# Channel order, first loads and first products of a two-stage layer on one core

## What is computed

```
qkv = xn @ W_qkv + b_qkv            # 512 -> 3 * 512, 16 heads of 32
q', k' = relu(q), relu(k), each times cos and sin of the position
kv = sum over rows of k'^T v        # per head, cos part and sin part
attn = (q' kv) / (q' sum(k') + 1e-4)
out1 = attn @ W_out + b_out
probs = softmax(xn @ choice_w^T)    # 8 experts
per batch and expert: its top 1024 rows -> silu(xn w1) w2, times the probability, added into the rows
```

## Time and profile before

| | us |
|---|---|
| median of 3 runs | 2501.93 (2501.14 to 2505.41) |
| the profiled execution, its time | 2501.82 |
| its span | 2500.0 |
| PE busy (matmul) | 2398.0 (96% of the span) |
| DVE busy | 1342.9 (54%) |
| ACT busy | 831.2 (33%) |
| POOL busy | 1078.0 (43%) |
| share of PE in the chain that ended last | 84% |

### The profile page before, as it was taken

The page is one execution under the profiler, slowest core; times in us unless marked ns, Lnnn a source line. Parts: engine busy times, 40 slices in busy tenths (PEclk is TensorE's granted clock), DMA queues, the critical chain, the costliest instruction groups (busy, mean ns, idle before and its releaser), DMA issues.

```text
span 2500.0 us, 34669 instructions
## 1 busy us (share of the span) xinstructions
PE 2398.0 (96%) x12544; PEld 2012.5 (80%) x12544; DVE 1342.9 (54%) x2654; ACT 831.2 (33%) x1458; POOL 1078.0 (43%) x959
## 2 busy tenths in 40 slices
PE   8999999999999999999999999998998999999898
PEld 7889988898999887777777787787787787787677
DVE  7777777687787795434335245245245344335331
ACT  4545544445454552222213213223223222223111
POOL 0100034200002565664565565565566566466541
PEclk9999999999999999999999999999999999999999
DMA  7555434455544455224224224323323323332222
GB/s 197 160 134 135 109 54 74 69 136 151 134 118 83 60 89 123 49 41 111 48 46 107 50 48 94 56 51 78 76 49 75 77 51 77 72 50 47 37 39 30
DMA packets 125947, 205.38 MB, mean 82 GB/s; under 512 B 28264, under 2 KB 53480, under 8 KB 125552
## 3 DMA queue, kind: packets, MB, share of 16 engines
q0 software_dynamic: 57088, 118.02, 26.5%
q1 hardware_dynamic: 68720, 85.42, 11.6%
HBM read 119.22 MB, written 100.93 MB: 88 GB/s over the span
## 4 chain that ended last, share of the span: by engine, by line
PE 84%; issue 6%; DVE 5%; another core or an unknown queue 2%; DMA 1%; ACT 1%; POOL 0%; POOLq 0%; DVEq 0%; SPq 0%; ACTq 0%
PE ps L1355 27%; PE ps L1357 26%; PE ps L1356 26%; PE ps L1448 2%; DVE h_lo L1322 1%; PE ps L1585 1%; DVE h_hi L1320 1%; DMA xo<-in_L_attn_x_dram 1%; PE ps L1382 1%; DMA normed_rows<-xo 0%; DVE one_lo L907 0%; ACT hf L773 0%; DVE stats L811 0%; DVE w_lo L1326 0%
## 5 line engine op out<-in xcount | busy, mean ns | idle before, releaser
L461 POOL DMA_INDIRECT rows<-normed_rows,idx_row x512 | 539.0, 1053 | 156.5 <-issue 156.5
L1355 PE MATMUL ps<-w_hi,h_hi 128*128 128x512 f32 x1024 | 412.7, 403 | 42.2 <-DVE h_lo L1322 21.0
L571 POOL DMA_INDIRECT out_dram<-y,idx x128 | 227.1, 1774 | 482.1 <-ACT y L793 480.0
L1355 PE MATMUL ps<-xi_hi,w_hi 128*128 128x512 f32 x1024 | 407.4, 398 | 8.5 <-issue 8.3
L1356 PE MATMUL ps<-w_lo,h_hi 128*128 128x512 f32 x1024 | 406.6, 397 | 5.8 <-issue 5.7
L1357 PE MATMUL ps<-w_hi,h_lo 128*128 128x512 f32 x1024 | 406.2, 397 | 4.6 <-issue 4.4
L1320 DVE CAST h_hi<-hf 128x512 fp32r<-128x512 f32 x256 | 111.3, 435 | 556.6 <-issue 292.2
L1356 PE MATMUL ps<-xi_lo,w_hi 128*128 128x512 f32 x1024 | 403.0, 394 | 1.6 <-issue 1.6
L1357 PE MATMUL ps<-xi_hi,w_lo 128*128 128x512 f32 x1024 | 401.5, 392 | 0.0
L773 ACT ACTIVATE hf<-ps 128x512 f32<-128x512 f32 x256 | 153.0, 598 | 678.5 <-PE ps L1357 437.6
L1355 PEld LDWEIGHTS ps<-w_hi,h_hi 128*128 128x128 f32 x1024 | 196.9, 192 | 96.8 <-issue 30.4
(11 more groups left out here) (176 smaller groups left out, 4117.3 us busy)
## 6 DMA issues: line engine op xcount, KB each, us to landing
xo<-in_L_attn_x_dram SPq DMA_DIRECT2D x32, 512.0 KB, 4.6
normed_rows<-xo SPq DMA_DIRECT2D x32, 512.0 KB, 4.9
out_dram<-bo POOLq DMA_DIRECT2D x16, 1024.0 KB, 9.1
out_dram<-xo POOLq DMA_DIRECT2D x64, 256.0 KB, 3.9
w_raw<-in_L_ffn_w_dram SPq DMA_DIRECT2D x32, 512.0 KB
w_raw<-in_L_ffn_w_dram SPq DMA_DIRECT2D x8, 2048.0 KB, 9.4
xn<-normed_rows SPq DMA_DIRECT2D x96, 128.0 KB, 2.5
rows<-normed_rows,idx_row POOLq DMA_INDIRECT x512
```

Source lines behind the costliest of these rows:

```text
L461: nc.gpsimd.indirect_dma_start(rows[:, tt, a, :], None, pieces[:, :], bass.IndirectOffsetOnAxis(ap=idx_row[:, b, tile, a:a + 1], axis=0)). ...
L571: nc.gpsimd.indirect_dma_start(of[:, :], bass.IndirectOffsetOnAxis(ap=idx[:, u * TPB + tt:u * TPB + tt + 1], axis=0), y[:, tt, :], None, c ...
L1355: nc.tensor.matmul(dst, a_hi, b_hi, start=start, stop=False, skip_group_check=True)
```

## The change

Channel c now lies in block k = c mod 4 at partition c div 4, so four neighbouring rows of a weight matrix belong to one partition, and each matrix is one transfer to 128 partitions. The two transposes on DVE read, and the write of xn scatters, in steps of that order: DVE reads every fourth element (16 bytes apart) where it read runs of 32, and `norm_rows` writes neighbouring elements 512 bytes apart.

The rest is order. The 19 increments leave SP and go to the engines that wait on them, x is loaded as two tiles and a half, Wk comes before the table and the biases, and q's bias has its own semaphore. At the start the statistics of half 1 and its normalisation move between the casts of weights; TensorE turns tiles 0 and 1, makes the left halves of the q products (256 columns) with tiles 2 and 3 turned between, and then the right halves, in banks 5, 6, 3 and 4. In block 0 of batch 0 the normalisation of block 1's half 0 moves from before the first tile to behind it.

```diff
-            for signal in (mm_done, kv_done, vv_ready, q_read, k_read, v_read, lg_read, o_raw, otr_done, out_done, fin, list_pe, idx_ready,
-                           silu_done, h_ready, down_done, y_ready):
-                sp.sem_inc(signal, AHEAD)
-            sp.sem_inc(prob_stored, DMA_AHEAD)
-            sp.sem_inc(wo_free, NBLK // 2 - 1)
...
-                for i in range(HPG):
-                    sp.dma_start(raw_weights(part)[i * HD:(i + 1) * HD, :, :],
-                                 w_qkv[i * P:(i + 1) * P, part * D:(part + 1) * D].rearrange("(k j) d -> j k d", j=HD)
-                                 ).then_inc(w_in[part], 16)
...
-            load_x(0, 0)
+                sp.dma_start(raw_weights(part), w_qkv[:, part * D:(part + 1) * D].rearrange("(p k) d -> p k d", k=KD)
+                             ).then_inc(w_in[part], 16)
...
+            for tt, landed in ((0, x_first), (1, x_in[0])):
+                sp.dma_start(x_half[0][:, tt, :], xf[tt * P:(tt + 1) * P, :]).then_inc(landed, 16)
             load_x(0, 1)
             sp.dma_start(ident, consts[:, C_IDENT:C_BLOCK]).then_inc(ident_in, 16)
             sp.dma_start(ch_rows, choice_w[:, :]).then_inc(ch_in, 16)
             load_weights(Q)
-            sp.dma_start(con[:, C_BLOCK:C_END], consts[:, C_BLOCK:C_END]).then_inc(table_in, 16)
             load_weights(V)
...
+            load_weights(K)
+            sp.dma_start(con[:, C_BLOCK:C_END], consts[:, C_BLOCK:C_END]).then_inc(table_in, 16)
+            sp.dma_start(bk[:, :], b_qkv[D:2 * D].rearrange("(a d) -> a d", a=1).to_broadcast([P, D])).then_inc(con_in, 16)
...
-                for i in range(HPG):
-                    sp.dma_start(w1_raw[i * HD:(i + 1) * HD, :, :],
-                                 w1[bass.ds(e, 1), i * P:(i + 1) * P, :].rearrange("e (k p) f -> p (e k) f", p=HD)
-                                 ).then_inc(w1_in, 16)
+                sp.dma_start(w1_raw[:, :, :], w1[bass.ds(e, 1), :, :].rearrange("e (p k) f -> p (e k) f", k=KD)
+                             ).then_inc(w1_in, 16)
...
+            for signal in (q_read, v_read, lg_read, fin, silu_done, y_ready):
+                act.sem_inc(signal, AHEAD)
             sqrt(0, 0)
-            sqrt(0, 1)
             def q_weights(m):
                 sl = slice(m * P, (m + 1) * P)
...
-            turned_hi(0, 0, None, 4)
-            turned_hi(0, 1, None, 5)
+            turned_hi(0, 0, None, X_BANKS[0])
+            turned_hi(0, 1, None, X_BANKS[1])
+            q_weights(1)
             act.wait_ge(ch_turned, 1)
             nc.scalar.copy(wq_hi[:, :, 3 * D:3 * D + E], ch).then_inc(ch_hi_ready, 1)
-            q_weights(1)
-            turned_hi(0, 2, None, 6)
-            turned_hi(0, 3, None, 7)
+            sqrt(0, 1)
             q_weights(2)
             q_weights(3)
+            turned_hi(0, 2, None, X_BANKS[2])
+            turned_hi(0, 3, None, X_BANKS[3])
...
                 def first_block(n):
                     q_out(n, 0, 0, 5, 1)
-                    q_out(n, 0, 1, 6, 2)
                     if n == 0:
                         kv_weights(K)
-                    q_out(n, 0, 2, 5, 3)
+                    q_out(n, 0, 1, 6, 2)
+                    q_out(n, 0, 2, FIRST_Q[2] if n == 0 else 5, 3)
                     q_out(n, 0, 3, 4, 4)
-                    sqrt(n + 1, 0)
+                    if n > 0:
+                        sqrt(n + 1, 0)
+                    else:
+                        act.wait_ge(table_in, 16)
...
                         k_high(n, t)
+                        if n == 0 and t == 0:
+                            sqrt(n + 1, 0)
...
-                            xn[:, 2 * s + tt, :].rearrange("p (k i j) -> p i k j", k=KD, i=HPG),
-                            src[:, tt, :].rearrange("p (i k j) -> p i k j", k=KD, i=HPG), mv[:, s, tt, 0:1],
+                            xn[:, 2 * s + tt, :].rearrange("p (k c) -> p c k", k=KD),
+                            src[:, tt, :].rearrange("p (c k) -> p c k", k=KD), mv[:, s, tt, 0:1],
...
                     xT_raw.rearrange("p k (a r) -> p a k r", a=HPG),
-                    xn[:, t, :].rearrange("p (a k j) -> p a k j", a=HPG, k=KD)).then_inc(pieces_turned, 1)
+                    xn[:, t, :].rearrange("p (a j k) -> p a k j", a=HPG, k=KD)).then_inc(pieces_turned, 1)
...
-                                    rows[:, tt, :, :].rearrange("p a (k j) -> p a k j", k=KD)
+                                    rows[:, tt, :, :].rearrange("p a (j k) -> p a k j", k=KD)
...
-            norm_half(0, 0, 0, False)
-            norm_half(0, 1, 0, False)
+            for signal in (vv_ready, k_read, o_raw, idx_ready, h_ready):
+                dve.sem_inc(signal, AHEAD)
...
+            dve.wait_ge(x_first, 16)
+            tile_stats(0, 0)
+            dve.wait_ge(x_in[0], 16)
+            tile_stats(0, 1)
+            half_stats(0)
+            dve.wait_ge(x_in[1], 16)
+            tile_stats(1, 0)
+            norm_rows(0, 0, 0, False)
+            tile_stats(1, 1)
             q_weights(0)
-            turned_lo(0, 0, 4)
-            turned_lo(0, 1, 5)
+            turned_lo(0, 0, X_BANKS[0])
+            turned_lo(0, 1, X_BANKS[1])
+            half_stats(1)
             dve.wait_ge(ch_hi_ready, 1)
             nc.vector.tensor_tensor(wq_lo[:, :, 3 * D:3 * D + E], ch, wq_hi[:, :, 3 * D:3 * D + E].bitcast(F32),
                                     ALU.subtract)
             q_weights(1)
-            turned_lo(0, 2, 6)
-            turned_lo(0, 3, 7)
+            norm_rows(0, 1, 0, False)
             q_weights(2)
+            turned_lo(0, 2, X_BANKS[2])
+            turned_lo(0, 3, X_BANKS[3])
+            q_weights(3)
             norm_store(0)
-            q_weights(3)
             norm_store(1)
...
                 n_first = b * NBLK
-                norm_half(n_first + 1, 0, 2 * b + 1, False)
+                if b > 0:
+                    norm_half(n_first + 1, 0, 2 * b + 1, False)
                 for t in range(TPB):
...
                     k_low(n_first, t)
                     if t == 0:
+                        if b == 0:
+                            norm_half(n_first + 1, 0, 2 * b + 1, False)
                         norm_stats(n_first + 1, 1)
...
+            for signal in (mm_done, kv_done, otr_done, out_done, list_pe, down_done):
+                pe.sem_inc(signal, AHEAD)
             pe.wait_ge(ident_in, 16)
-            for t in range(TPB):
-                turn_x(0, t, 4 + t)
-                if t == 1:
-                    pe.wait_ge(ch_perm_ready, 1)
-                    for k in range(KD):
-                        last = nc.tensor.transpose(ch[:, k, :], ch_perm[:, k * P:(k + 1) * P], ident[0:E, 0:E])
-                    last.then_inc(ch_turned, 1)
+            for t in range(2):
...
                 q_half(0, 5, 0)
+                if b == 0:
+                    pe.wait_ge(w_ready, 2)
+                    q_half(1, FIRST_Q[1], 0)
+                    for t in range(2, TPB):
+                        turn_x(0, t, X_BANKS[t])
+                    for m in range(2, KD):
+                        pe.wait_ge(w_ready, m + 1)
+                        q_half(m, FIRST_Q[m], 0)
                 pe.wait_ge(xT_ready, b * NBLK * TPB + TPB)
                 def block(n, first):
                     pe.wait_ge(xT_ready, (n + 1) * TPB)
                     q_half(0, 5, 1)
-                    if first:
-                        pe.wait_ge(w_ready, KD)
+                    if not first:
+                        kv(n - 1, TPB - 1)
+                    if first and b == 0:
+                        for m in range(1, KD):
+                            q_half(m, FIRST_Q[m], 1)
                     else:
-                        kv(n - 1, TPB - 1)
-                    pe.wait_ge(lg_read, AHEAD + n * TPB)
-                    q_rest(1, 6)
-                    pe.wait_ge(q_read, AHEAD + n * KD + 1)
-                    q_rest(2, 5)
-                    pe.wait_ge(k_read, AHEAD + n * TPB)
-                    if first and b > 0:
-                        pe.wait_ge(fin, AHEAD + b * NT)
-                        pe.wait_ge(rank_out, b)
-                    q_rest(3, 4)
+                        pe.wait_ge(lg_read, AHEAD + n * TPB)
+                        q_rest(1, 6)
+                        pe.wait_ge(q_read, AHEAD + n * KD + 1)
+                        q_rest(2, 5)
+                        pe.wait_ge(k_read, AHEAD + n * TPB)
+                        if first:
+                            pe.wait_ge(fin, AHEAD + b * NT)
+                            pe.wait_ge(rank_out, b)
+                        q_rest(3, 4)
```

More of the change, by code:

```diff
@@ L54 @@
 VW = P + HPG
-CON_LOADS = 3
+CON_LOADS = 2
 HALF = D // 2
@@ L58 @@
 AHEAD, DMA_AHEAD = 1, 16
+X_BANKS = (0, 1, 2, 7)
+FIRST_Q = (5, 6, 3, 4)
 XN_TILES = B * NBLK * TPB
@@ L427, in _ @@
                 load_w2(e + 1)
-            sp.wait_ge(w1_in, HPG * 16 * E)
+            sp.wait_ge(w1_in, 16 * E)
             sp.wait_ge(w2_in, 16 * E)
```

(25 more changed lines are left out.)

26 lines of the change are left out of this document (14 added, 12 removed).

## The result

The changed kernel takes 2540.18 us, median of 6 runs (2537.2 to 2556.68), against 2505.43 for the kernel before beside it (2501.14 to 2509.13): ratio 1.0155, 95% interval 1.0126 to 1.0184. Its profiled execution took 2539.84 us with a span of 2538.0, 38.0 longer than before's span. The forecast was 2503.5.

What follows compares the result with a forecast made beforehand. The prediction took TensorE's stream as the bound. 2501.8 us, plus 1.1 net for the start and 0.5 for strided transposes, gave 2503.4 (2503.5 in terms of the median), range 2498.8 to 2507.0.

Steps and rivals of the forecast that it cites:

- something in stage 3 shifts: Unnamed case: something in stage 3, such as gathers beside a faster w1, shifts either way by several us; chance 0.05.
- Wq at 8.8, by the rate of x: Start: Wq, loaded at x's 380 GB/s, is there at 8.8 us instead of about 12.
- The third rival: Start: loads to 128 partitions no faster than 223 GB/s, Wq at 11 us, 2506 us in all; chance 0.06.
- First turning at 8.1: Start: TensorE turns the first tile of x at 8.1 us, 4.3 to 4.4 us after statistics can begin.
- First product at 11.5: Start: TensorE's first q product begins at 11.5 us, 4.5 earlier than before.
- q phase 14.0 us: First block's q products: 14.0 us instead of 12.13, from added turning, a longer slow pace and a wait for Wq.
- V at 25.5: First block: the first v product starts at 25.5 us instead of 28.16, a gain of 2.66.
- V + 32.0, and 0.7 for the writes: Block 1's right half: DVE's list ends 32.0 us after the first v product, strided writes add 0.7: 58.2 against 57.09.
- Writes at 0.72: `norm_rows` on DVE: each strided write of xn takes 0.72 us, between 0.54 and 0.83.
- Transposes +0.4: DVE's transposes in stages 1 and 3: reading every 16 bytes adds 0.4 us each, between 0 and 0.44.
- Coming through, +0.5: Blocks 2 and 3 of batch 0: DVE's gaps do not hide all the slower transposes; +0.5 us reaches the total.
- The strided transposes bound stage 1: Rival: slower transposes exceed the 1.18 us a steady tile leaves free on DVE; +20 us, 2522; chance 0.05.

Runs made afterwards that it cites:

- the second run of the norm first: Changed kernel, 24 increments at TensorE's start, second block's norm before the first tiles, first `norm_rows` before the wait for half 1: 2497.85 us, ratio 0.9962.
- the one that has increments directly ahead of the loop: Changed kernel with 24 unread semaphore increments directly ahead of TensorE's expert loop: 2497.57 us in one run, on a chip where the kernel before takes 2505.58.
- 24 and 52: Changed kernel with that many unread semaphore increments at the start of TensorE's program: 2380.92 and 2383.36 us, the kernel before at 2375.59.
- 64 and 76: Kernel before with that many unread semaphore increments at TensorE's start: 2523.18 us (2505.58 without, on that chip) and 2402.66 us (2375.59 without).

## Why the prediction was wrong

The forecast of 2503.5 us is 37 too low. The step that failed is the one that costs stage 3 at nothing. It asked what the change does to stage 3's data (slower transposes "off the path", single transfers of w1 "issued long before their casts") and, since no instruction of TensorE changes there, nothing of its code. What changed is where they lie. The case "something in stage 3 shifts" had 0.05 and no place in the trace; its place is the loop's head, its price 4.3 us a pass in this trace (3.7 to 4.3 in those of the other kernels that wait at the second product). Nothing in before's trace shows the border, though the order of instructions shows that 36 products were added ahead of the loop, and the queue of instruction packets (98 of them) that the loop is fetched anew.

Point by point:
- *SP's first load near 0.8:* 0.75. Right.
- *Wq at 8.8, by the rate of x:* cast at 9.28. Nearly right; from 8 to 9 us the loads to 128 partitions moved 397 GB/s, where the four transfers had 223. The third rival's cause is wrong, though V and block 1's right half came out where it put them (28 and 60.7), for other reasons.
- *First turning at 8.1:* 9.57, as before. Wrong. "The added statistics and its wait for half 1" were sized at 0.2 us; the rows of half 1 came at 6.48, and the reciprocal, whose root was there at 5.5, stood behind them until 7.09.
- *First product at 11.5:* 13.00, 1.5 late like the turning. That wait is only part of it: with `norm_rows` ahead of it (the second run of the norm first, 11.94) the first product gained 0.5 and the turning, at 8.44, 0.6; and one multiplication of the same chain, 0.16 us before, took 0.71 here (0.16 to 0.86 in the other runs, which stays unexplained).
- *q phase 14.0 us:* 15.33. The slow pace was sized at +0.3: 19 of the products took 0.21 us instead of 0.12, in place of 9 before, +1.0, with the granted clock at 1.00 throughout. The wait for Wq's last part was sized at 0.7 and took 0.75.
- *V at 25.5:* 28.33, the sum of the two. So the first block had nothing in hand.
- *V + 32.0, and 0.7 for the writes:* block 1's right half at V + 33.1 (61.45) against V + 28.7 before, a difference of 4.4; the prediction had 32.7 less 28.9, 3.8 (it took V of before at 28.16, and V was at 28.38). The three waits for VectorE, 3.7 us, are the "some 3 us" expected. Right in kind and nearly in size. With V 2.8 late it made the start +4.3 instead of +1.1.
- *Writes at 0.72:* 848 ns, beyond the 0.83 of the bound.
- *Transposes +0.4:* 707 to 1092 ns, +0.39. Right; the rule on lines of 16 bytes that the prediction weighed, from the Trainium skill, page "SBUF — State Buffer", section "Door 1: The DMA port swizzle", agrees. *Coming through, +0.5:* the prediction's own numbers, 1.6 less 1.1 in each of two blocks, give 1.0. From the fourth tile's keys to stage 3 the changed kernel loses 0.4 against the trace of before, and the kernels with the new layout take 885.8 to 886.2 us there (without the one that has increments directly ahead of the loop), those with the old one 885.0 to 885.5. Right in size.
- *The strided transposes bound stage 1:* they did not; TensorE is busy 843.3 of the 845 us from 100 to 945.
- *Wrong if the stretch from 945 on changes by more than 2 us:* it did, by 33, and this was the sign to follow.

## What to carry to other kernels

An edit that only adds instructions ahead of a loop can slow the loop. Where a long loop's head shows a wait on issue that the kernel before did not have, compare that place first, and try some harmless instructions at the start of that engine's program before judging the edit itself. Try more than one count: 24 and 52 took the loss away from the changed kernel, 64 and 76 brought it to the kernel before, and 24 directly ahead of the loop cost 2.9 us of their own. A step that is moved out of an engine's idle time costs nearly its whole length in the list behind it (3.7 of 4.0 us here).

## What was not expected of the hardware

- TensorE waits 2.3 to 3.8 us ahead of the second product of a pass where a border of the instruction supply falls there, 1.5 us on average where it falls behind the seventh, and not at all where it falls behind the 19th (a place worked out from the number of increments); a product counts as two instructions.
- The place of a loop decides whether its code is fetched again: 35 instruction packets against 98. Where no wait results, the time between them is small: 1.7 us of stage 3 in two traces, and not measurable in the kernel before (1.0007, 0.9979 to 1.0034).
- The granted clock stood at 0.50 for some 3 us behind the wait of 2.60 us, and behind four of the seven waits in that trace; behind the one of 2.48 us it stayed at 1.00. Behind those at the 8th product it differed too: 1.00 in the pass with a wait of 1.63, 0.50 in the next one with 1.96.
- A write of 512 elements to steps of 512 bytes takes 848 ns instead of 544, a transpose that reads every 16 bytes 1092 instead of 707.
